# Destination degrees of a graph network counted in the second gather pass instead of while the sources are ordered

## The reference

```python
# block 0: degrees of the source nodes
deg = segment_sum(ones, row)                    # row = src
deg_inv_sqrt = where(deg > 0, rsqrt(max(deg, 1)), 0)
out = segment_sum(x[col] * (deg_inv_sqrt[row] * deg_inv_sqrt[col])[:, None], row)
# block 1: relational: out[dst] += (x @ W[rel])[src]
# block 2: edge MLP, sums over the sources, node MLP
# block 3: two GCN convolutions with self loops: degrees of the destinations
deg = segment_sum(ones, dst) + 1
dinv = rsqrt(deg)
h = relu(conv(x, W1) + b1); out = conv(h, W2) + b2 + x @ W_emb + b_emb
```

## Time and profile before

| | us |
|---|---|
| median of three runs | 5206.31 |
| lowest and highest | 5196.57, 5220.39 |
| span of the profiled execution | 6179.1 |

### The profile page before, as it was taken

The page is one execution under the profiler, slowest core; times in us unless marked ns, Lnnn a source line. Parts: engine busy times, 40 slices in busy tenths (PEclk is TensorE's granted clock), DMA queues, the critical chain, the costliest instruction groups (busy, mean ns, idle before and its releaser), DMA issues. The chain is left out here.

```text
span 6179.1 us, 72632 instructions
## 1 busy us (share of the span) xinstructions
PE 3566.1 (58%) x19811; PEld 2738.2 (44%) x19811; DVE 2253.1 (36%) x4940; ACT 1380.4 (22%) x3101; POOL 3107.2 (50%) x2834
## 2 busy tenths in 40 slices
PE   3333362466756663455547667977993345717448
PEld 2111121465722322454336554676772344716447
DVE  7444592233555651221701101243452122503128
ACT  0000000000133440111401014633440122303125
POOL 2555506676166776777365533000115777377733
PEclk8555575555576776776555558999996676858769
DMA  3000041111145663111524345565563111211114
GB/s 104 2 2 2 10 149 35 37 46 39 56 188 208 232 245 131 20 22 22 195 66 114 101 115 158 175 201 175 196 231 135 21 22 22 101 24 19 23 26 149
DMA packets 311485, 589.50 MB, mean 95 GB/s; under 512 B 178785, under 2 KB 180702, under 8 KB 292960
## 3 DMA queue, kind: packets, MB, share of 16 engines
q1 hardware_dynamic: 146819, 465.93, 21.3%
q0 software_dynamic: 87808, 66.01, 5.9%
q10 hardware_dynamic: 76506, 53.12, 2.6%
HBM read 286.68 MB, written 310.95 MB: 97 GB/s over the span
## 5 line engine op out<-in xcount | busy, mean ns | idle before, releaser
L1303 PE MATMUL e_ring<-e_msgs,e_hot 128*128 x6272 | 1162.3, 347 | 1182.0 <-issue 1124.2
L1303 PEld LDWEIGHTS e_ring<-e_msgs,e_hot 128*128 128x128 f32 x6272 | 1077.1, 248 | 1270.4 <-issue 1264.6
L1028 POOL DMA_INDIRECT e_msgs<-y,index_D x784 | 880.2, 1123 | 402.7 <-issue 226.9
L1147 DVE TENSOR_TENSOR e_hot<-iota,keys_D 128x2048 f32<-128x2048 f32 x147 | 337.1, 2293 | 1472.9 <-remote 732.5
L603 POOL DMA_INDIRECT list_D<-d_place,d_target x392 | 456.5, 1165 | 318.7 <-DVEq L557 202.0
L1028 POOL DMA_INDIRECT e_msgs<-y,index_S x392 | 400.5, 1022 | 377.9 <-DVE index_S L1133 194.6
L603 POOL DMA_INDIRECT list_S<-s_place,s_target x392 | 390.8, 997 | 363.4 <-DVEq L557 248.0
L1627 POOL DMA_INDIRECT m_far<-x,index_S x392 | 390.0, 995 | 353.0 <-DMA pairs_by_edge<-m_far 225.4
L1028 POOL DMA_INDIRECT e_msgs<-x_by_relation,index_D x392 | 446.5, 1139 | 170.2 <-issue 110.9
L1777 PE MATMUL m_ring<-rows,m_hot 128*128 x1568 | 374.3, 423 | 213.4 <-issue 211.2
L2453 POOL TENSOR_TENSOR n_sq<-n_cent 128x1792 f32<-128x1792 f32 x14 | 44.4, 3175 | 826.4 <-DVE n_cent L2348 826.4
(11 more groups left out here) (386 smaller groups left out, 5706.0 us busy)
## 6 DMA issues: line engine op xcount, KB each, us to landing
x_by_relation<-d_stage SPq DMA_DIRECT2D x98, 1024.0 KB
m_keyrow<-keys_by_step SPq DMA_DIRECT2D x49, 512.0 KB
rows<-pairs_by_edge SPq DMA_DIRECT2D x49, 512.0 KB
messages<-rows SPq DMA_DIRECT2D x98, 256.0 KB
rows<-messages SPq DMA_DIRECT2D x49, 512.0 KB, 4.0
sums<-m_stage ACTq DMA_DIRECT2D x98, 256.0 KB, 3.8
n_in<-sums SPq DMA_DIRECT2D x14, 1792.0 KB
s_xc<-x_padded SPq DMA_DIRECT2D x28, 448.0 KB, 3.8
```

What stands on the lines that cost most here:

```text
L1028: pool.indirect_dma_start(out=msgs[:, (i % HELD) * D:(i % HELD + 1) * D], out_offset=None, in_=source, in_offset=bass.IndirectOffsetOnAxis ...
L1147: nc.vector.tensor_tensor(hot[g % 2][:, :, :], bc(nodes[:, 0:P].unsqueeze(1), [P, GS, P]), bc(order["keys"][:, g * GS:(g + 1) * GS].unsque ...
L1303: mm = nc.tensor.matmul(ring[:, bass.ds(bucket, step)], hot[g % 2][:, k, :], moved, start=False, stop=False, skip_group_check=True)
```

## The change

In `order_sources` the second counting loop is gone. The 98 counts are now of the sources alone, two in each of the first 49 quads; the inverse root of the source degrees moves behind quads 50 and 52, and the 28 scalings behind two of every three quads from 54 on. The step table comes last. `present` gets a tile of its own, and only one PSUM bank is used for degrees.

In `stair_pass`, a new argument `count` makes 98 counts of the given digits, two in each group: VectorE's rows behind its release of the group, TensorE's eight matmuls behind the group's 16, into the first spare bank. Behind the last group the inverse root gives `dinv`. e1 gets this argument and is no longer `wide`. Since one destination table now serves a pass that isn't wide and two that are, the table always holds the bucket shifted for 64 columns, and a wide pass shifts it down by 15 instead of 16. `high_dst` and `low_dst` are kept through the program.

```diff
@@ Sorter.dve_table
-        self.step(dve, nc.vector.tensor_scalar(self.within[:, :], self.within[:, :], 22 if "halves" in order else 23, None,
+        self.step(dve, nc.vector.tensor_scalar(self.within[:, :], self.within[:, :], 22, None,
@@ order_sources, VectorE
             for q in range(QUADS):
                 sort.dve_rank(dve, q)
-                degree_hots(q)
+                if q < QUADS // 2:
+                    degree_hots(2 * q)
+                    degree_hots(2 * q + 1)
                 if (q + 1) % UQ == 0:
                     sort.dve_unit(dve, q // UQ)
-
-            dve.wait_ge(sem("prior"), 1)
-            sort.dve_passed(dve)
-            sort.dve_table(dve)
-            present = sort.rank
-            scaled = 0
-            for q in range(QUADS):
-                degree_hots(QUADS + q)
-                if q == 2:
+                if q == QUADS // 2 + 1:
+                    dve.wait_ge(s_deg, QUADS)
...
-                if q >= 8 and q % 3 == 2 and scaled < HCHUNKS:
+                if q >= QUADS // 2 + 5 and q % 3 != 2 and scaled < HCHUNKS:
...
             assert scaled == HCHUNKS
-            dve.wait_ge(s_deg, 2 * QUADS)
-            nc.vector.tensor_scalar(K["dinv"][:, :], p_deg[1][:, 0:T], 1.0, None, ALU.add).then_inc(s_max, 1)
-            dve.wait_ge(s_root, 2)
-            nc.vector.reciprocal(K["dinv"][:, :], K["dinv"][:, :])
+            dve.wait_ge(sem("prior"), 1)
+            sort.dve_passed(dve)
+            sort.dve_table(dve)
@@ order_sources, TensorE
                 sort.pe_lookup(pe, q)
-                degree_sums(q)
+                if q < QUADS // 2:
+                    degree_sums(2 * q)
+                    degree_sums(2 * q + 1)
             sort.pe_steps(pe)
-            for q in range(QUADS):
-                degree_sums(QUADS + q)
@@ stair_pass, VectorE, in each group behind its release
+                if count is not None:
+                    for m in (2 * g, 2 * g + 1):
+                        if m >= 2:
+                            dve.wait_ge(s_deg, m - 1)
+                        for j in range(QUAD):
+                            t = m * QUAD + j
+                            nc.vector.tensor_scalar(hot_high[m % 2][:, j, :], K["iota16"][:, 0:P],
+                                                    count_high[:, t:t + 1], None, ALU.is_equal)
+                            op = nc.vector.tensor_scalar(hot_low[m % 2][:, j, :], K["iota16"][:, :],
+                                                         count_low[:, t:t + 1], None, ALU.is_equal)
+                        op.then_inc(s_counted, 1)
@@ stair_pass, VectorE, behind the last group
+            if count is not None:
+                dve.wait_ge(s_deg, QUADS)
+                nc.vector.tensor_scalar(K["dinv"][:, :], p_deg[:, 0:T], 1.0, None, ALU.add).then_inc(s_degree, 1)
+                dve.wait_ge(s_root, 1)
+                nc.vector.reciprocal(K["dinv"][:, :], K["dinv"][:, :])
@@ stair_pass, TensorE
-                        at[k] >> 16, 0, (RING * BL - 1) * step,
+                        at[k] >> (15 if wide else 16), 0, (RING * BL - 1) * step,
...
                 mm.then_inc(s_group, 1)
+                if count is not None:
+                    for m in (2 * g, 2 * g + 1):
+                        pe.wait_ge(s_counted, m + 1)
+                        for j in range(QUAD):
+                            mm = nc.tensor.matmul(p_deg[:, 0:T], hot_high[m % 2][:, j, :], hot_low[m % 2][:, j, :],
+                                                  start=m == 0 and j == 0, stop=m == QUADS - 1 and j == QUAD - 1)
+                        mm.then_inc(s_deg, 1)
@@ gnn
-        stair_pass(nc, "e1", K, orders["D"], 2, xw, None, fresh=listing["D"], start=x1, rows=rows, normed=(x2, x2t), wide=True)
+        stair_pass(nc, "e1", K, orders["D"], 2, xw, None, fresh=listing["D"], start=x1, rows=rows, normed=(x2, x2t),
+                   count=(flat(K["high_dst"]), flat(K["low_dst"])))
```

More of the change, by code:

```diff
@@ L635, in order_sources @@
         p_v = [ps(f"p_v{h}", [P, 512]) for h in range(2)]
-        p_deg = [ps(f"p_deg{n}", [P, 512]) for n in range(2)]
+        p_deg = ps("p_deg", [P, 512])
+        p_base = ps("p_base", [P, 512])
         parts = [slice(c * PARTT, (c + 1) * PARTT) for c in range(PARTS)]
@@ L663, in order_sources @@
         block = inner.enter_context(nc.Block())
-        keys = ((flat(K["high_src"]), flat(K["low_src"])), (flat(K["high_dst"]), flat(K["low_dst"])))
+        high, low = flat(K["high_src"]), flat(K["low_src"])
         HCHUNKS = T // HC
@@ L829, in _ @@
                 sort.act_hott(act, q)
[L830 to L833, removed]
+                if q == QUADS // 2 + 2:
+                    act.wait_ge(s_max, 1)
+                    nc.scalar.activation(degree[:, :], degree[:, :], ACT.Sqrt).then_inc(s_root, 1)
         inner.close()
@@ L840, in stair_pass @@
 def stair_pass(nc, label, K, order, column, source, sums, fresh=None, sort=None, extra=None, turned=None,
-               start=None, scale=None, rows=None, normed=None, conv=None, finish=None, wide=False):
+               start=None, scale=None, rows=None, normed=None, conv=None, finish=None, wide=False, count=None):
     with ExitStack() as ctx:
@@ L942, in stair_pass @@
                            spare[0:1], spare[1:3], spare[0])
+        if count is not None:
+            count_high, count_low = count
+            hot_high = [sb(f"hot_high{h}", [P, QUAD, P], F16) for h in range(2)]
+            hot_low = [sb(f"hot_low{h}", [P, QUAD, T], F16) for h in range(2)]
+            p_deg = spare[0]
+            s_counted = sem("counted")
+            s_deg = sem("deg")
+            s_degree = sem("degree")
+            s_root = sem("root")
         begins = start is not None or rows is not None
@@ L1289, in _ @@
                     order["table"][0:1, g * GS:(g + 1) * GS], [mybir.EngineType.PE], min_val=0,
-                    max_val=((RING * BL - 1) * step << 16) + (HELD - 1) * D,
+                    max_val=((RING * BL - 1) * D << 16) + (HELD - 1) * D,
                     skip_runtime_bounds_check_because="both parts are masked to their rings before they are stored")
@@ L1470, in _ @@
                 act.wait_ge(s_extra, 48)
+            if count is not None:
+                act.wait_ge(s_degree, 1)
+                nc.scalar.activation(K["dinv"][:, :], K["dinv"][:, :], ACT.Sqrt).then_inc(s_root, 1)
             if conv is not None:
@@ L2745, in sorted_by @@
             return sorting.enter_context(nc.sbuf_tensor(name, shape, dt))
-        for name in ("src", "dst", "rel", "ew", "high_src", "low_src", "high_dst", "low_dst"):
+        for name in ("high_dst", "low_dst"):
+            K[name] = sb(name, [P, QUAD, QUADS])
+        for name in ("src", "dst", "rel", "ew", "high_src", "low_src"):
             K[name] = sorted_by(name, [P, QUAD, QUADS])
```

16 lines of the change are left out of this document (7 added, 9 removed).

## The result

The changed kernel takes 5173.05 us (median; 5168.21 to 5179.76) where the kernel before takes 5203.59 on the same chip (5195.46 to 5230.36): a ratio over all runs of 0.9933, 95% interval 0.991 to 0.9955. By this ratio the change is worth -35 us, with -23 to -47 inside the interval (the two medians alone differ by 31 us); the forecast was -71. The direction was right, and the time lies in the range.

What follows compares the result with a forecast made beforehand. GpSimd's chains of 392 indirect DMAs were taken to set the pace, about level with VectorE in the ordering. Ordering -14 and second gather pass -57 gave -71 us, 5206 to 5135 us; range 5040 to 5225.

Steps and rivals of the forecast that it cites:

- the 973 us have to be somewhere: Whole kernel: the profiled span exceeds the median by 973 us, taken as a reason that late releases mostly belong to recording.
- R1: Rival, ordering of sources: TensorE's late releases occur in every execution, not just the recorded one; -160 us there; chance 0.25.
- late releases: Ordering of sources: VectorE waits 317.0 us for TensorE releases arriving 10 us and more late, taken as mostly recording.
- stall-free sum: Ordering of sources before the change: VectorE's recorded durations without the long waits, ending at about 602 us.
- Part A: Ordering of the sources: destination degrees leave it, its end goes from 602 to 588 us, -14 us (-39 to +14).
- Part B: Second gather pass (e1): narrow ring, added degree rows and longer end, -72 + 8 + 7 = -57 us (-72 to -35).
- (1): Second gather pass: the wide ring goes, the one-hot build reads one SBUF operand and stops holding gathers, -72 us.
- (2): Second gather pass: 784 pairs of degree rows added on VectorE beside gathers, +8 us (0 to 16).
- (3): Second gather pass: TensorE's groups with degree matmuls, 461 us against 478 us of gathers, hidden by 17 us.
- The tail: Second gather pass, behind the last gather: eight degree matmuls (2.6 us), then add, root and reciprocal (4 us), +7 us.
- R2: Rival, second gather pass: no shorter, as TensorE and VectorE pass work to and fro, 11 us a group; 5199 us; chance 0.15.
- R3: Rival, second gather pass: each degree row holds GpSimd for its whole length, 154 us held; 5281 us; chance 0.10.

Runs made afterwards that it cites:

- narrow_only: Kernel before with only the second gather pass made narrow (iota in PSUM), destination degrees still counted in the ordering: 5168.44 us, ratio 0.9904.
- order_only: Changed kernel with the second gather pass wide again and no destination count at all: 5214.31 us, ratio 0.9994 to the kernel before.
- no_dst_count: Changed kernel without the destination count, second gather pass still narrow: 5163.91 us, ratio 0.9898 to the kernel before.
- narrow_sbuf: Changed kernel with the second gather pass's one-hot build reading the nodes' iota from SBUF again: 5260.55 us, ratio 1.01 to the kernel before.
- one_count: Changed kernel with one source count per quad over all 98 quads, scalings behind them: 5157.28 us, ratio 0.9901 to the kernel before.

## Why the prediction was right and wrong, step by step

**What bounds the kernel.** Right in kind: a chain of 392 indirect DMAs, and GpSimd sets the pace in the ordering and in e1. Wrong in one number, the pitch (from one put to the next). I took 1.20 us, on the thought that the recording adds to the 0.30 us gap. The spans stand 1.8 to 2.0 us under the executions' own times, so nothing is added: the pitch is 0.971 + 0.30 = 1.27 us as the earlier trace rows said. The argument "the 973 us have to be somewhere" was fair, but I spread it over both the stalls and the gap, and the gap had no part in it.

**R1** fell: in all other traces VectorE's quads follow at about 2.7 us without late releases, and VectorE ends at 597.96. My stall-free sum had put that at 602. The forecast of about 440 for the changed kernel held as well: its VectorE ends at 437.5.

**Part A, -14 forecast, -3 to -5 measured.** The failing term is the end of the stage before. I set it at 602, VectorE's own end, with GpSimd alone at 595; GpSimd's last put starts 32 to 63 us later than that, because its puts are held by scalings and counting rows (33.9 to 64.4 us). The holding was left out of before, and only 8 us of it were put into after. So VectorE never bound the stage, and its 194 us were worth nothing. For after I had 108 + 14 x 33.6 + 2 + 8 = 588; measured are 108.9 for the first put (forecast 107.6) and 639.8 for the last: 392 x 1.27 = 498 and 33.7 held. By units (28 puts each, from the trace) the first five take about 39 us where 35.7 are the bare pitch, 3.5 us held over 14 counts, 0.25 us a count; the scalings hold the units after that; the last five are bare. That the forecast of -14 came within some 10 us of the measured change is luck: both of its ends were too early, 602 by 34 to 64 us and 588 by 60, and the errors cancel. Its range for this part also left the 8 us out at the lower end (563 in place of 571). Named correctly: a later first put, scalings always beside puts. Mis-sized: the counts at nothing, the scalings at 8, the pitch. Not foreseen: that the same holding was already in before, and there depends on the phase.

**Part B, -57 forecast, about -41 measured.** (1) -72 for the build's operand is the term of the sum that failed by its size: the mechanism is shown by narrow_only, order_only with no_dst_count, and narrow_sbuf, but it is worth -50. The 72 us came from the means of the disturbed execution, where a gather began earlier in its build (0.59 us in, held by 1.5 us, against 1.13 and 1.04). Both held gathers of the earlier trace rows already end 0.82 us after VectorE's step; I read the amount as a constant of the build, and it is set by the phase. (2) +8 for the degree rows beside gathers: 5 us measured (496.7 against 491.5). (3) TensorE hidden: right. 17 us of slack were forecast; in the trace TensorE waits 59.5 us for builds, and its groups follow the gathers at 10.1 us (496.7 / 49), not at the 9 to 9.5 that would have told of a pace of its own. The tail: +7 forecast, and +7.0 measured between last gather and first sum. Two rows of the changed kernel, the added degree and the first sum (the last gather starts at 2294.5; the earlier trace rows for before have 10.7 us between the two, the first undisturbed one 10.4):

```profile
2308.15 0.57 DVE L1204 TENSOR_SCALAR dinv<-e_spare 128x392 f32<-128x392 f32 x1 [6.67 <-PE e_spare L1329]
...
2311.89 1.96 DVE L1258 TENSOR_REDUCE e_mean<-rows 128x28 f32<-128x1792 f32 x1
```

Sum by the experiments: -50 (operand) -4 (counts leave) +9 to 11 (counts in e1) = -43 to -45; the two kernels compared directly give -35 (-23 to -47). The difference is within the intervals.

**R2** (e1 doesn't get shorter) fell: e1 is 47 us shorter, though TensorE, mostly at the lower clock, and VectorE do pass work to and fro.

**R3** (each degree row holds GpSimd for its whole length) fell as a sum. Had each of 784 pairs held GpSimd, e1 would be 154 us longer; 5 us are measured. The Trainium skill's page "SBUF — State Buffer", section "SBUF: two separate sides", gives the shared port as an exclusive lock for a whole instruction. For two SBUF operands the traces bear that out once the gather starts within the build: it waits for all that is left of it (1.84 of 2.27 us in narrow_sbuf), and a put lost 1.00 us to a 1.08 us scaling in before. For the counting rows (f16, one SBUF operand) a single put can lose 0.30 us beside a row of 0.31 us, which is as long as one row, but never the eight rows of a count together: per count the traces show 0.05 us beside gathers and 0.25 us beside puts. So what the traces refute is that every row beside a gather holds it, not that one row can.

What would have mended the forecast: a second profiled execution. Its 51 us for 72 and its last put at 657.6 in place of 756.4, without a wait but the first, would have corrected both wrong terms before anything was built. Short of that, a trace whose span is 19% over the timed median should have moved me to give held DMAs the same doubt as late releases.

**Open.** Why a count's rows hold a put five times as long as a gather (0.25 against 0.05 us) was not tried. The phase has a part in it: puts with counting rows alone beside them have a median of 1.268 us in one execution of the kernel before and 0.984 in another. Nor is it known why a scaling holds a put that is already 0.24 us under way, when a build does not hold a gather that is. What disturbed the first execution is unknown, and it never came back. Whether a good phase of scalings and puts can be had on purpose was not tried, as moving the operand to PSUM makes it needless. The puts of the destination list (mean 1.15 us, 68 of them over 1.3 us, some 73 us held in the undisturbed traces, changed kernel included) are held more than any chain treated here, and no run tried the cure on them.

## What to carry to other kernels

Where GpSimd issues indirect DMAs back to back and sets the pace, look at what VectorE reads beside them. Where one of its steps reads two operands from SBUF, put the broadcast one into PSUM: here the gathers then ran at their bare pitch, worth 50 us per pass of 392, more than all the rest of the change. Moving VectorE work off a stage whose chain is GpSimd's gave nothing that could be measured here (194 us moved, 3 to 5 us gained), and it costs where it delays the first DMA of the chain (11 us here, which one_count got back). Compare a profile's span with the timed runs before costing anything from it.

## What was not expected of the hardware

The same instruction holds a neighbour by different amounts: a one-hot build of 2.3 us held its gather by 1.04, 1.5 or 1.84 us, according to how far the build had come when the gather began, for the gather ended 0.82 to 0.83 us after the build in all of them. The same phase repeats through long stretches. In the kernel before the holding of puts by scalings and rows makes executions differ by 30 us (ends of the ordering 635.6 to 666.3). In the third and fourth pass a mean granted clock of 0.50 in place of 0.73 cost no time at all.
